# Segment-max pass of a graph network: one TensorE signal per round from a drain, selection two rounds behind, node stages three chunks later

## The reference, cut to what matters

```python
Wd, Ws, ww = (Wm[:H], Wm[H:2 * H], Wm[2 * H])
msgs = z[edge_dst] @ Wd + z[edge_src] @ Ws + edge_weight[:, None] * ww[None, :] + bm
agg = jax.ops.segment_max(msgs, edge_dst, num_segments=n)
agg = jnp.where(deg[:, None] > 0, agg, jnp.zeros((), dtype=z.dtype))
W1a, W1b = (W1[:H], W1[H:])
hidden = jax.nn.relu(z @ W1a + agg @ W1b + b1)
return hidden @ W2 + b2
```

## Time and profile before

| | |
|---|---|
| Median of 3 runs | 3869.01 us (3853.34 to 3870.36) |
| Span of the profiled execution | 3851.9 us |
| Max pass in it (first to last selection) | 1987.7 to 3211.2 us |
| TensorE busy, whole span | 3125.2 us (81%) |
| VectorE, ScalarE, GpSimd busy | 38%, 25%, 61% |
| TensorE's granted clock, whole span / 1985 to 3212 us | 0.818 / 0.61 |

### The profile page before, as it was taken

One profiled execution on the slowest core, in us unless ns is written; L12 is line 12 of the kernel. 1 busy time (PEld: TensorE's weight loads), 2 busy tenths in 40 slices (PEclk: granted clock), 3 DMA queues, 4 the chain that ended last, 5 costly groups with the idle time before them and its releaser, 6 DMA issues.

```text
span 3851.9 us, 54329 instructions
## 1 busy us (share of the span) xinstructions
PE 3125.2 (81%) x21070; PEld 2150.6 (56%) x21070; DVE 1459.7 (38%) x3223; ACT 958.7 (25%) x2512; POOL 2340.9 (61%) x2327
## 2 busy tenths in 40 slices
PE   3788788878889888888857787878878787999898
PEld 2444444455557677777735555555656564555454
DVE  6555555223222111111224444544444443333333
ACT  2555455122222011010122222322222232000000
POOL 3666662666662665666446666666666662777775
PEclk7899999899999999999955665665665667999899
DMA  5444444655555666666433343433444337666564
GB/s 150 162 160 166 167 149 156 200 175 185 190 181 172 193 193 188 198 193 201 144 112 103 108 116 101 119 102 112 112 127 127 111 113 253 211 226 218 195 225 144
DMA packets 278767, 621.83 MB, mean 161 GB/s; under 512 B 60077, under 2 KB 188649, under 8 KB 270953
## 3 DMA queue, kind: packets, MB, share of 16 engines
q1 hardware_dynamic: 171944, 372.56, 28.5%
q0 software_dynamic: 104832, 244.47, 22.5%
q10 hardware_dynamic: 1728, 1.25, 0.1%
HBM read 477.62 MB, written 140.45 MB: 160 GB/s over the span
## 4 chain that ended last, share of the span: by engine, by line
PE 56%; another core or an unknown queue 15%; issue 13%; DVE 7%; ACT 6%; DMA 3%; SPq 1%; DVEq 0%; POOL 0%; ACTq 0%; POOLq 0%
PE banks L2056 27%; PE banks L1294 5%; PE banks L2077 4%; PE banks L554 3%; PE banks L2075 3%; PE banks L1283 3%; PE banks L1272 3%; PE banks L1274 1%; PE banks L529 1%; PE banks L2170 1%; PE banks L1154 1%; DMA ring_of_rows<-weight_parts 1%; ACT arena L2363 1%; ACT arena L1213 1%
## 5 line engine op out<-in xcount | busy, mean ns | idle before, releaser
L2056 PE MATMUL banks<-arena 128*128 128x384 bf16 (+1 forms) x9310 | 1557.1, 316 | 129.0 <-issue 114.3
L2056 PEld LDWEIGHTS banks<-arena 128*128 128x128 bf16 x9310 | 914.4, 100 | 618.0 <-issue 235.8
L516 POOL DMA_INDIRECT arena<-tab_l,ring_of_rows x831 | 808.4, 973 | 472.3 <-issue 286.3
L2121 POOL DMA_INDIRECT arena<-h_pieces,span_sources x450 | 435.8, 968 | 319.2 <-issue 108.3
L2121 POOL DMA_INDIRECT ring_of_rows<-message_pieces,span_sources x396 | 430.2, 1086 | 214.1 <-issue 98.0
L2121 POOL DMA_INDIRECT ring_of_rows<-x_pieces,span_sources x306 | 332.9, 1088 | 201.3 <-PE banks L2075 101.1
L1294 PE MATMUL banks<-arena 128*128 128x64 f32 x1662 | 349.8, 380 | 123.4 <-issue 123.0
L2101 DVE TENSOR_TENSOR arena<-iota_bf,span_targets 128x768 bf16<-128x768 bf16 x243 | 134.9, 556 | 822.3 <-remote 318.3
L2121 POOL DMA_INDIRECT ring_of_rows<-l_pieces,span_sources x306 | 300.7, 983 | 233.0 <-issue 71.8
L1294 PEld LDWEIGHTS banks<-arena 128*128 128x128 f32 x1662 | 315.9, 284 | 201.5 <-issue 190.4
L1388 DVE TENSOR_TENSOR_SCAN ring_of_rows<-arena,ring_of_rows,banks 128x512 f32<-128x512 bf16 x207 | 264.2, 1277 | 135.6 <-remote 57.7
(11 more groups left out here) (243 smaller groups left out, 3098.4 us busy)
## 6 DMA issues: line engine op xcount, KB each, us to landing
arena<-edge_counts SPq DMA_DIRECT2D x83, 896.0 KB
arena<-edge_counts SPq DMA_DIRECT2D x83, 672.0 KB
edge_counts<-arena SPq DMA_DIRECT2D x32, 1568.0 KB
typed_counts<-arena SPq DMA_DIRECT2D x27, 1568.0 KB
arena<-scan_mask SPq DMA_DIRECT2D x208, 128.0 KB
arena<-typed_counts SPq DMA_DIRECT2D x27, 896.0 KB
arena<-typed_counts SPq DMA_DIRECT2D x27, 672.0 KB
arena<-tab_l,ring_of_rows POOLq DMA_INDIRECT x831
```

Of the source, the lines that this page charges most:

```text
L516: k.nc.gpsimd.indirect_dma_start(k.RG3[:, i % p.ring, at:at + width], None, table, bass.IndirectOffsetOnAxis(ap=k.SRC[:, i:i + 1], axis=0) ...
L2056: t = T.matmul(k.bank[i % N_SUMS][:, 0:rows.shape[-1]], counts[:, s, :], rows, start=s == 0 and n == 0, stop=s == NT - 1 and n == len(term ...
L2121: G.indirect_dma_start(k.rows[p.layer][s % n], None, k.pieces[p.layer], bass.IndirectOffsetOnAxis(ap=k.SRCG[:, at:at + 1], axis=0)).then_i ...
```

## The change

On TensorE, selection moves to two rounds behind (`SELECT_LAG = 2`), the typed counts move ahead of `turn_back`, and none of the four steps of a round signals by itself any more. At the end of each round stands `T.drain()`, which waits until TensorE has finished what it was given, and then raises one semaphore, `l2_round`. All consumers of `l2_turned` (after the first two chunks), `l2_product`, `l2_back` and `typed_counted` (after the first 8 units) wait for the right count of `l2_round`. Two rounds with only a selection and a drain stand at the end. The node stages still signal by themselves. `l2_slots` asks three chunks more of the pass before a node step, so each step stands three chunks later and the last 12 steps of the loop fall behind it. On VectorE the one-hot columns are made one chunk later and taken columns two chunks later.

```diff
-            while done < end and (NEWEST[done] if regular else min(done, N_ET - 1)) < (c * CH if c < NCH else N_ET):
+            while done < end and (NEWEST[done] if regular else min(done, N_ET - 1)) < ((c - (SELECT_LAG + 1) * regular) * CH if c < NCH else N_ET):
...
+def round_done(k, c):
+
+    return k.sem("l2_round"), c + 1
+
+
+def chunk_turned(k, c):
+    return (k.sem("l2_turned"), 1) if c < 2 else round_done(k, c - 2)
+
+
+def chunk_selected(k, c):
+    return round_done(k, c + SELECT_LAG)
+
+
+def units_counted(k, n):
+    return (k.sem("typed_counted"), n) if n <= UNITS else round_done(k, n - UNITS - 1)
...
-        if c:
-            select(c - 1)
+        if c >= SELECT_LAG:
+            select(c - SELECT_LAG)
         nodes(k.slots[c][1])
-        turn_back(c)
-        nodes(k.slots[c][2])
         if typed_unit(c):
             tensor_typed_counts(k, *typed_unit(c))
+        nodes(k.slots[c][2])
         nodes(k.slots[c][3])
-    select(NCH - 1)
+        t = turn_back(c)
+        T.drain().then_inc(round_done(k, c)[0], 1)
+    for c in range(NCH, NCH + SELECT_LAG):
+        t = select(c - SELECT_LAG)
+        T.drain().then_inc(round_done(k, c)[0], 1)
...
-        V.wait_ge(k.sem("l2_turned"), c + 1)
+        V.wait_ge(*chunk_turned(k, c))
...
-            one_hots(c + 1)
+        one_hots(c)
...
-        if c:
-            take(c - 1)
-    take(NCH - 1)
+        if c >= SELECT_LAG + 1:
+            take(c - SELECT_LAG - 1)
+    for c in range(NCH - SELECT_LAG - 1, NCH):
+        take(c)
...
-        A.wait_ge(k.sem("l2_back"), c + 1)
+        A.wait_ge(*round_done(k, c))
...
-    A.wait_ge(k.sem("typed_counted"), UNITS * i + u + 1)
+    A.wait_ge(*units_counted(k, UNITS * i + u + 1))
...
-            G.wait_ge(k.sem("l2_turned"), (i - AHEAD) // CH + 1)
+            G.wait_ge(*chunk_turned(k, (i - AHEAD) // CH))
```

More of the change, by code:

```diff
@@ L51 @@
 HOT_RING = 3
+SELECT_LAG = 2
 END_MARGIN, TILE_MARGIN = 6, 4
@@ L372, in __init__ @@
         self.stages = REGULAR if regular else STAGES
-        self.product = k.sem(f"{layer}_product")
+        self.product = None if regular and layer == "l2" else k.sem(f"{layer}_product")
         self.added = k.sem(f"{layer}_added")
@@ L1273, in turn_messages @@
         T.wait_ge(k.sem(f"load_mask_{c % MASKS}"), 32 * (c // MASKS + 1))
-        T.matmul(bank[:, 0:len(tiles) * P], k.WW9, k.W9[c % MASKS][:, 0:len(tiles) * P], start=False,
-                 stop=True).then_inc(k.sem("l2_turned"), 1)
+        return T.matmul(bank[:, 0:len(tiles) * P], k.WW9, k.W9[c % MASKS][:, 0:len(tiles) * P], start=False, stop=True)
     def turn_back(c):
@@ L1294, in select @@
             t = T.matmul(window(k, c), k.RG3[:, i % p.ring, 0:H], k.HOT[:, c % HOT_RING, q, :], start=i == tiles[0], stop=i == tiles[-1])
-        t.then_inc(p.product, 1)
+        return t
     turn_messages(0)
     turn_messages(1)
+    T.drain().then_inc(k.sem("l2_turned"), 1)
     fold_turn()
@@ L1369, in take @@
     def take(c):
-        V.wait_ge(p.product, c + 1)
+        V.wait_ge(*chunk_selected(k, c))
         if c:
@@ L1546, in max_sync_l2 @@
         load_messages(k, p, a, b)
-    S.wait_ge(p.product, NCH)
+    S.wait_ge(*chunk_selected(k, NCH - 1))
     for a, b in SOURCES[1]:
```

15 lines of the change are left out of this document (8 added, 7 removed).

## The result

| | before | after |
|---|---|---|
| Median of 4 runs each | 3861.18 us (3841.0 to 3870.36) | 3903.61 us (3891.15 to 3909.34) |
| Ratio, with its 95% interval | | 1.013 (1.0099 to 1.0161) |
| Span of the profiled execution | 3851.9 us | 3894.8 us |
| TensorE busy, idle, per round (2300 to 2900 us) | 4.69, 1.25 us | 4.87, 1.19 us |
| One round there | 5.94 us | 6.06 us |

The change makes the kernel slower by 1.3%. Faster was forecast, with about 3752 us. Where the executions of one kernel fell into a faster and a slower group, the times and ratios here are those of the faster group (the trace of the kernel before with 32 gathers in experiment 7 is of a slower execution).

What follows compares the result with a forecast made beforehand. TensorE was taken as the bound, GpSimd next at 4.99 us: 4.69 + 1.25 - 0.60 - 0.40 + 0.30, plus 0.10, is 5.34 us a round; -125 + 8 gives about 3752 us. Range 3690 to 3945, likeliest case 3680 to 3815.

Steps and rivals of the forecast that it cites:

- Selection two rounds behind: TensorE's wait before the selection, for ScalarE's copy, goes except for rare cases: -0.60 us a round.
- Counting: TensorE's wait before the counting, for ScalarE's casts, nearly goes if the drain's signal is prompt: -0.40 us of 0.44 a round.
- the sign that I had named for being wrong altogether: The max pass keeps its length while TensorE's idle time before selection is gone.
- Four signals less, one drain more: At each round's end on TensorE, emptying the array and restarting costs 0.30 us a round, 62 us in all.
- Rival A: The drain makes TensorE itself wait out the lateness every round: 6.24 us a round, 3939 us, slower; chance 0.28.
- Rival B: The drain's signal is late but TensorE goes on, and the counting pays: 5.84 us a round, 3856 us; chance 0.15.
- Clock: TensorE's mixture of low and high clock in the max pass, granted mean 0.61, is left as it is.
- C: Rival: a stop every round keeps TensorE's clock low, 5.72 us a round, 3831 us, a little faster; chance 0.07.
- Gathers: GpSimd's lead falls from four rounds to three at no cost, but its own 4.99 us a round is the floor.
- Scan, one-hots, taking: VectorE's work in the max pass, 2.7 us a round, stays hidden.
- The end, +8: Behind the last chunk, 12 node steps add 5 us and one more selection round 3 us.

Runs made afterwards that it cites:

- experiment 7: Both kernels on one chip: before 3850.85 us, changed 3895.57; with only the max pass's first 32 gathers, before 3476.52, changed 3563.66.
- Experiment 2: Kernel before with selection two rounds behind, its four signals kept and no drain: 3881.43 us, ratio 0.9997.
- Experiment 1: Changed kernel with the drain taken out, the round's last product giving the one signal: 3893.94 us, ratio 1.0012.
- experiment 8: Changed kernel with only the first 32 gathers, without the drain 3534.24 us (ratio 0.9115) and with it 3577.47 us (0.9233), on one chip.
- experiment 3: Kernel before with a drain added at the end of each round and nothing else changed: 4034.91 us, ratio 1.0393.
- experiment 6: Changed kernel with 64-row gathers, plain copies by GpSimd, or plain copies by SyncE: 3352.12, 3302.22, 3259.84 us, where the kernel before takes 3363.

## Why the prediction was wrong

**The step that failed** is the gain: "Selection two rounds behind" with -0.60 and "Counting" with -0.40 us a round. Both took it that a wait is saved when what it waits for gets more time. The runs show that the wait moves to another place. Experiment 2 removes the wait before the selection alone, and the round stays at 5.93 us. Experiment 1 has the whole new order without the drain, for which the sum without its 0.30 gives 5.04 us; measured are 5.94, with 0.99 us before the counting and 0.10 before the selection. In the changed kernel both waits are 0.0, and 1.17 us stand behind the drain in their place. So the 1.00 us of gain came to nothing. I had taken the two waits for the only places at which lateness can be paid, and the sign that I had named for being wrong altogether came true. What I had put behind that sign, that something other than lateness sets the pace, is neither shown nor excluded: with the gathers away the lateness goes and the round falls to 4.19 us, but half of that fall is busy time at a higher clock.

**"Four signals less, one drain more", +0.30.** What stands at the drain is much more than that: 1.17 us of idle time and 0.18 us of busy time that no longer overlaps (4.87 against 4.69), 1.35 us a round. Of this a prompt drain's price is 0.18 + 0.25 = 0.43 us; the other 0.9 us is lateness. But that lateness is paid without a drain too, so what the drain adds is less: 0.1 to 0.2 us a round against experiment 1, 0.21 us in experiment 8, and 0.7 to 0.8 us where the kernel before gets it (experiment 3). As the order gains nothing, this and the longer end are the loss. A mean of the lateness was to be had from the profile before: in 2300 to 2900 us ScalarE's copy starts 1.3 us, in the mean of 101 rounds, behind the recorded end of turning back or behind ScalarE's own work before it, whichever is later, and at most 7.6 us. The 148.4 us of the earlier trace rows are ScalarE's idle time before 37 copies, which is not the same: it counts also the time before turning back had ended.

**Rival A is what the trace of the changed kernel shows.** Its round was 6.24 us and its point of decision a drain of 1.25 us; measured are 6.06 us in the stretch and 6.09 over the pass, with 1.35 us. Its sign, a gap of over 1.2 us, was missed by little (1.17). Its argument was the right one: idling doesn't hurry the late signals. What stood against it, that products are fed steadily during the lateness, is true and is no argument, since feeding goes on only as long as nobody asks whether the array is through. What A lacked is that the saved waits would not have been saved without the drain either. The rule of the Trainium skill that stood beside A ("Perfetto Trace Analysis", section "Tensor Engine Instruction (MATMUL, LD_WEIGHTS)") has the end of a product's record as an estimate, and this trace agrees: drains end up to 5.3 us behind it. That the acknowledgement by PSUM is what comes late, no run here shows.

**Rival B is what experiment 1 shows**, where the signal is as late as any other and TensorE goes on. Its price for the counting was +0.2 and measured is +0.55, with -0.52 at the selection; its 3856 us are 0.3% under the kernel before, and measured is 0.1% over it.

**Clock.** 0.62 against 0.61 in the stretch; leaving it alone was right, and C has nothing for it. **Gathers.** Three rounds of lead were enough: GpSimd's issue time is 110.8 us as before, and its 95.5 us of other waiting is for the drain. It never was the bound here, and is so where nothing is late (experiment 6). **Scan, one-hots, taking** stayed hidden, as forecast: VectorE is busy 263 of 600 us and TensorE waits for it nowhere in the rows.

**The end, +8.** Measured +13.6 us. The 12 steps were priced at 5 us as if they nearly fitted in the room that was there, but the message loads, which set the end, stand behind them: from the last selection's end to these loads it is 17.9 us (3244.62 to 3262.53) against 7.5 before, 10.4 us more. The selection rounds behind the last turning back take 5.0 us against 1.5 before (3209.96 to 3211.50), 3.5 more where I had 3.

**What stays open.** Why TensorE's signals come late while gathers go out, why in clusters, and what sets 5.94 us a round so firmly that the lag does not move it and six products less hardly do. One loop that would give such a firmness is the single bank of turning back, with its late signal to ScalarE and back every round; a second bank for it was not tried. Which part of a gather does it (its rows, its indices, GpSimd's queue) is open too, as experiment 6 fell on a chip without lateness. And that the lateness belongs to the chip is inferred: on that chip only kernels with changed gathers have a trace, but the kernel before is 13% faster there.

## What to carry to other kernels

A late semaphore and a late drain come and go together here, with the gathers. Before a drain takes the place of signals, measure over many rounds how long after its producer's last recorded end a consumer starts; the mean of that, not its best case, is about what will stand at the drain, on top of the 0.3 to 0.45 us of a prompt one. What the drain adds to a round is that less the waits it takes the place of: 0.1 to 0.2 us in one order of this kernel, 0.7 to 0.8 in the other. And where an engine's signals are late, taking away one wait moves it to the next single-buffered hand-over: look for the loop as a whole, and try the lag alone (a few lines here) before building on its gain.

## What the runs showed of the hardware

- TensorE's signals came up to 7.6 us behind the recorded end of their product (kernel before, copies in 2300 to 2900 us; 6.8 us in the earlier trace rows) while GpSimd gathered rows. In kernels that stop gathering after 32 of 831, 209 of 211 drains ended within 0.03 us of it, in three traces on three chips, and the two late ones of each stand while those gathers go out.
- Products that wait for nothing are still fed during the lateness (2.0 us of them in the earlier trace rows, from 2400.16 to 2402.17).
- A drain with nothing to wait for costs 0.29 to 0.30 us of a round at the high clock (2.66 and 2.67 us without it, 2.96 with it), and 0.21 us of a round by the difference of whole kernels (43 us over 208).
- Without the late signals TensorE's granted clock in 1990 to 2850 us was 0.76 against 0.60, and its busy time a round 3.83 against 4.67 us.
- Chips differ: the same kernel before takes 3850 to 3890 us (medians) in five sets of runs, on four chips at least, and 3363 us on one more, where no late signal was seen in four traces of kernels with changed gathers.
